# Feed-forward with blockwise rounding: weights rounded inside the expert loop, norm and input by quarters, pair loop written out

## The reference

```python
def fp4_quant_dequant(x):                 # blocks of 16 along the last axis
    scale = max(max(abs(xb)) / 6, 1e-12)
    idx = searchsorted(_MID, abs(xb / scale))
    return _GRID[idx] * sign(xb / scale) * scale
def fp4_linear(x, w): return einsum('bsk,nk->bsn', quant(x), quant(w))
x = x + ga * linear_attention(h)
h = layernorm(x) * (1 + cb) + sb
gate = fp4_linear(h, w_gate)              # w_gate, w_up: 352 x 128
y = fp4_linear(h, w_up)
x = x + gb * fp4_linear(silu(gate) * y, w_down)   # w_down: 128 x 352
```

## Time and profile before

| what | value |
|---|---|
| median of 3 runs | 1143.52 us (1142.25 to 1144.01) |
| the profiled execution | 1143.78 us |
| its span | 1142.0 us |
| PE busy | 884.3 us (77%) |
| DVE busy | 734.3 us (64%) |
| ACT busy | 453.7 us (40%) |
| POOL busy | 411.9 us (36%) |
| chain that ended last | PE 46%, DVE 23%, DMA 7%, POOL 7%, SP queue 6%, ACT 5%, issue 5% |

### The profile page before, as it was taken

One profiled execution on the slowest core, in us unless ns is written; L12 is line 12 of the kernel. 1 busy time (PEld: TensorE's weight loads), 2 busy tenths in 40 slices (PEclk: granted clock), 3 DMA queues, 4 the chain that ended last, 5 costly groups with the idle time before them and its releaser, 6 DMA issues.

```text
span 1142.0 us, 22164 instructions
## 1 busy us (share of the span) xinstructions
PE 884.3 (77%) x8587; PEld 671.1 (59%) x8587; DVE 734.3 (64%) x1571; ACT 453.7 (40%) x748; POOL 411.9 (36%) x447
## 2 busy tenths in 40 slices
PE   2484679999999999874689989999937850467774
PEld 1243668888888888653356656666615840254553
DVE  6683426555555655336687887888858768876664
ACT  4850123333333333245545565655633223222221
POOL 5552003333334333245223353334442056223232
PEclk8696889999999999896799999999978985578776
DMA  7075112233233323620000000000000000000000
GB/s 132 0 191 169 41 35 58 65 91 72 62 85 74 70 60 92 160 53 3 1 1 2 1 2 1 1 1 1 1 0 1 1 20 0 0 9 10 18 18 18
DMA packets 69608, 46.37 MB, mean 41 GB/s; under 512 B 35056, under 2 KB 60856, under 8 KB 68792
## 3 DMA queue, kind: packets, MB, share of 16 engines
q1 hardware_dynamic: 52776, 24.75, 9.7%
q0 software_dynamic: 8032, 19.11, 6.4%
q10 hardware_dynamic: 8704, 1.19, 0.6%
HBM read 30.05 MB, written 12.06 MB: 37 GB/s over the span
## 4 chain that ended last, share of the span: by engine, by line
PE 46%; DVE 23%; DMA 7%; POOL 7%; SPq 6%; ACT 5%; issue 5%; ACTq 0%; POOLq 0%; DVEq 0%
PE PS L1029 7%; PE PS L1125 5%; PE PS L1126 5%; PE PS L1127 5%; PE PS L1049 4%; PE PS L1009 3%; PE PS L1033 3%; PE PS L1010 3%; PE PS L1261 2%; SPq L336 2%; PE PS L1277 2%; DMA REG<-inverse_sums 2%; DVE HB L1682 2%; DVE REG L1479 2%; ACT REG L687 1%
## 5 line engine op out<-in xcount | busy, mean ns | idle before, releaser
L1460 DVE TENSOR_REDUCE MX<-PS 128x2 f32<-128x512 f32 x256 | 171.4, 686 | 172.2 <-PE PS L1010 170.6
L766 ACT ACTIVATE REG<-PS 128x1024 f32<-128x1024 f32 x128 | 131.5, 1027 | 242.2 <-PE PS L1033 239.4
L1029 PE MATMUL PS<-XX,TB 96*128 96x64 f16 x2048 | 160.0, 246 | 7.3 <-DMA XX<-NEG 4.5
L1009 PE MATMUL PS<-TM,YY 128*128 128x256 f16 x512 | 129.8, 285 | 32.8 <-DMA YY<-REG 15.2
L1029 PEld LDWEIGHTS PS<-XX,TB 96*128 96x128 f16 x2048 | 133.5, 120 | 22.8 <-issue 12.8
L608 POOL TENSOR_TENSOR HH<-HB,HH 128x512 f16<-128x512 f32 x64 | 75.6, 1181 | 171.2 <-ACT HH L813 171.2
L1010 PE MATMUL PS<-KM,YY 128*128 128x256 f16 x512 | 126.8, 279 | 0.0
L1682 DVE SCALAR_TENSOR_TENSOR HB<-PS,SG 128x512 f32<-128x512 f32 x128 | 87.5, 684 | 50.7 <-ACT SG L841 50.7
L841 ACT ACTIVATE SG<-PS 128x512 f32<-128x512 f32 x128 | 76.2, 595 | 110.3 <-PE PS L1127 110.0
L1033 PE MATMUL PS<-XX,KC 97*128 97x128 f16 x1024 | 107.8, 229 | 0.0
L1125 PE MATMUL PS<-XH,XX 128*128 128x512 f16 x256 | 98.8, 386 | 9.1 <-DVE HB L1682 8.9
(11 more groups left out here) (235 smaller groups left out, 1704.3 us busy)
## 6 DMA issues: line engine op xcount, KB each, us to landing
REG<-inverse_sums POOLq DMA_DIRECT2D x60, 128.0 KB, 2.9
YY<-queries_content ACTq DMA_DIRECT2D x224, 4.0 KB
KC<-keys_strips SPq DMA_DIRECT2D x16, 192.0 KB
keys_strips<-REG POOLq DMA_DIRECT2D x12, 224.0 KB, 8.0
R<-in_L_attn_x SPq DMA_DIRECT2D x32, 64.0 KB, 3.4
out<-R SPq DMA_DIRECT2D x64, 32.0 KB, 1.6
queries_position<-REG POOLq DMA_DIRECT2D x2, 960.0 KB, 12.9
queries_content<-REG POOLq DMA_DIRECT2D x2, 960.0 KB, 17.7
```

Of the source, the lines that this page charges most:

```text
L766: A(P[jt][:, 1024 * up:1024 * up + 1024].rearrange("p (k x) -> p k x", k=2), ST[u % 2], ACT.Exp).then_inc(exp_done, 1)
L1009: mm(o, yp[:, a], TM[p][:, 31 - a:31 - a + T], start=True, stop=False)
L1029: mm(o_pos[:, a], TB[p][0:96, y0:y0 + 128], xp[0:96, 8 * bank + a], start=(a == 0), stop=False, skip_group_check=True)
L1460: nc.vector.tensor_reduce(MX[h % 2][:, 2 * kk:2 * kk + 2], banks[4 + kk % 2].rearrange("p (a j) -> p a j", a=2), AX_X, ALU.max)\
```

## The change

- FN, WGU, WD1 and buffers for rounding the weights move into parts of YY that are free once layer 0's attention is done. GpSimd clears FN after the last normalise of attention, and SP loads the weights then instead of after layer 1's attention.
- VectorE rounds the weights in 16 pieces beside the expert loop (ten in block 1 from step 6, six in block 3 from step 10). TensorE transposes them in block 4 (steps 2 and 8) into banks 6 and 7, ScalarE copies them out (steps 6 and 10).
- Statistics, root, centring, scaling and shift go by quarters of eight tiles; VectorE now does the shift too. The input of quarters 0 and 1 is rounded ahead of the pairs, that of 2 and 3 in pieces between the steps of the first pairs.
- The input tiles are transposed two at a time within the pair loop, into bank 7, and go straight from there to XT; R1 isn't used.
- The pair loop is written out on all engines. TensorE's order is gate_and_up(m+1), hidden_transposes(m-1), down(m-2), input_transposes(m+3). HT has two buffers, both down products of a pair lie in bank 6, and GpSimd does output(m-3) behind scale_hidden(m).

The diff, cut (lines "# sync" and so on name the engine):

```diff
+        FN = YY[:, 3 * N + 1800:3 * N + 1800 + 2 * (768 + FF)].bitcast(F32)
+        YF = YY[:, 0:3 * N].bitcast(F32)
...
-        FN = sb("FN", [128, 6 * 128 + FF], F32, ff)
-        WGU = sb("WGU", [128, 2, FF], F32, ff)
-        WD1 = sb("WD1", [128, 3, 128], F32, ff)
-        HT = sb("HT", [128, 2, 3, 128], F32, ff)
+        HT = [sb(f"HT{j}", [128, 2, 3, 128], F32, ff) for j in range(2)]
 # sync
-            sp.wait_ge(l_od, 8)
             sp.wait_ge(zeroed, 15)
...
-            with sp.Fori(0, NT // 4) as c:
+            for c in range(NT // 4):
 # gpsimd
             for h in range(H - 1):
                 sums_to_dram(h)
                 normalise(h)
+            gp.wait_ge(max_mm, 16 * H)
+            gp.memset(FN, 0.0).then_inc(zeroed, 1)
...
-            residual(l_mul, R2, [CT[j][:, :] for j in range(2)], l_od)
-            gp.wait_ge(l_od, 8)
-            gp.memset(FN[:, :], 0.0).then_inc(zeroed, 1)
-            inverse_root(5)
-            shifted(3, HN3, MOD[1][:, 3, :], pre_ready)
...
-            scale_hidden(0, 0)
-            with gp.Fori(0, PAIRS // 2 - 1) as c:
-                for v in range(2):
-                    scale_hidden(2 * c + v + 1, 1 - v)
-                    output(2 * c + v, v)
-            scale_hidden(PAIRS - 1, 1)
-            output(PAIRS - 2, 0)
-            output(PAIRS - 1, 1)
+            for q in range(4):
+                linear_residual(2 * q)
+                linear_residual(2 * q + 1)
+                if q:
+                    quarter_root(5, q - 1)
+            quarter_root(5, 3)
+            scale_input(0)
+            scale_input(1)
+            for m in range(PAIRS):
+                scale_hidden(m)
+                if m in (2, 5):
+                    scale_input(2 + m // 5)
+                if m >= 3:
+                    output(m - 3)
+            for m in range(PAIRS - 3, PAIRS):
+                output(m)
 # scalar
+                elif tc == 4 and k in (6, 10):
+                    feed_weights(k // 4 - 1)
...
+            def stationary(m):
+                v = m % 2
+                act.wait_ge(f_xtr, m + 1)
+                if m >= 2:
+                    act.wait_ge(f_gu, m - 1)
+                A(XT[v][:, :, :], banks[7][:, 0:256].rearrange("p (u t) -> p u t", u=2), ACT.Copy).then_inc(f_xt, 1)
...
+            for q in range(3):
+                centre_tiles(5, HN3, range(8 * q, 8 * q + 8))
+            stationary(0)
+            stationary(1)
+            centre_tiles(5, HN3, range(24, 32))
             silu_gate(0)
+            stationary(2)
+            for m in range(PAIRS + 2):
                 if m + 1 < PAIRS:
                     silu_gate(m + 1)
+                if 1 <= m <= PAIRS:
+                    evacuate_hidden(m - 1)
+                if m >= 2:
+                    evacuate_output(m - 2)
                 if m + 3 < PAIRS:
+                    stationary(m + 3)
 # tensor
+                elif tc == 4 and k in (2, 8):
+                    feed_transposes(k // 8)
...
+            def input_transposes(m):
+                pe.wait_ge(h_ready, 24 + 2 * (m // 4) + 2)
+                if m:
+                    pe.wait_ge(f_xt, m)
+                for u in range(2):
+                    last = tr(banks[7][:, 128 * u:128 * u + 128], XQ[:, 2 * m + u, :], ident)
+                last.then_inc(f_xtr, 1)
...
-            with pe.Fori(0, PAIRS // 2 - 1) as c:
-                for v in range(2):
-                    gate_and_up(2 * c + v + 1, 1 - v)
-                    hidden_and_down(2 * c + v, v)
+            pe.wait_ge(l_mul, 8)
+            input_transposes(0)
+            input_transposes(1)
+            gate_and_up(0)
+            input_transposes(2)
+            for m in range(PAIRS + 2):
+                if m + 1 < PAIRS:
+                    gate_and_up(m + 1)
+                if 1 <= m <= PAIRS:
+                    hidden_transposes(m - 1)
+                if m >= 2:
+                    down(m - 2)
+                if m + 3 < PAIRS:
+                    input_transposes(m + 3)
 # vector
+            def feed_weights():
+                ve.wait_ge(ld_ff, 80)
+                for part, (lo, nb) in enumerate(((0, 48), (768, FF // 16))):
+                    w = FN[:, lo:lo + 16 * nb].rearrange("p (k s) -> p k s", s=16)
+                    t = [b[:, 0:16 * nb].rearrange("p (k s) -> p k s", s=16) for b in (WS0, WS1)]
+                    if part:
+                        ve.wait_ge(f_w, part)
+                    yield from quantised(w, t[0], t[1], [v[:, 0:nb] for v in WAM], norm, f_wround)
+                    ve.wait_ge(f_wround, part + 1)
+                    TT(w, t[0], WAM[2][:, 0:nb].unsqueeze(2).to_broadcast([128, nb, 16]), ALU.mult).then_inc(f_w, 1)
+                    yield
...
+                elif tc == 1 and k >= 6 or tc == 3 and k >= 10:
+                    next(weights)
...
-            scaled(3, HN3, MOD[1][:, 4, :])
...
+            def hidden(m):
+                v = m % 2
+                ve.wait_ge(f_sg, m + 1)
+                if m >= 2:
+                    ve.wait_ge(f_ht, m - 1)
+                elif m == 1:
+                    ve.wait_ge(h_ready, 24 + 4)
+                TT(HQ[v][:, :, :], SGP[:, :, :], gate_up[:, :, 1], ALU.mult).then_inc(f_h, 1)
+                yield
+                ve.wait_ge(f_h, m + 1)
+                yield from quantised(HQ[v][:, :, :].rearrange("p u (k s) -> p (u k) s", s=16), *pair_buffers[v][0:2],
+                                     pair_buffers[v][2:], hidden_step, f_round)
...
             for c in range(4):
+                linear_gate(c)
+            for _ in feed_statistics(0):
+                pass
+            for c in range(4, 6):
+                linear_gate(c)
+            for _ in feed_statistics(1):
+                pass
+            for c in range(6, 8):
+                linear_gate(c)
+            for piece in (feed_norm(0), feed_statistics(2), feed_input(0), feed_norm(1), feed_statistics(3), feed_input(1)):
+                for _ in piece:
+                    pass
+            behind = itertools.chain(feed_norm(2), feed_input(2), feed_norm(3), feed_input(3))
+            for m in range(PAIRS):
+                for _ in hidden(m):
+                    next(behind, None)
```

More of the change, by code:

```diff
@@ L7 @@
+import itertools
 from contextlib import ExitStack
@@ L705, in projected @@
                 A(*natural(c, 0), ACT.Identity, bias=VEC3[:, kind:kind + 1]).then_inc(high_done, 1)
-            def centre(k, src, dst, done, before=0):
-                for n in range(NT):
-                    if n % (NT // 2) == 0:
-                        act.wait_ge(rstd_ready, 17 + n // (NT // 2))
-                    last = A(dst[:, n, :], src[:, n, :], ACT.Identity, bias=LN[:, 3, n:n + 1], scale=LN[:, 2, n:n + 1])
-                    if n % 4 == 3:
-                        last.then_inc(done, 1)
             for q in range(3):
@@ L950, in _, with transposes @@
             tr(banks[7][:, 0:128], WN[:, 4, :], ident).then_inc(pe_prep, 1)
[L952 to L960 removed]
+            def transposes(c):
+                pe.wait_ge(h_ready, c + 1)
+                if c >= 2:
+                    pe.wait_ge(t_evac, c - 1)
+                for j in range(4):
+                    last = tr(banks[4 + c % 2][:, 128 * j:128 * j + 128], HN[:, 4 * c + j, :], ident)
+                last.then_inc(t_done, 1)
             def project(c):
@@ L1111, in linear_transposes, with feed_transposes @@
                 last.then_inc(t_done, 1)
+            def feed_transposes(part):
+                pe.wait_ge(f_w, part + 1)
+                if part == 0:
+                    pe.wait_ge(t_evac, 16 + 2)
+                    for w in range(2):
+                        for c in range(3):
+                            m = (128, 128, 96)[c]
+                            last = tr(banks[6 + w][:, 128 * c:128 * c + m], FN[0:m, 384 * w + 128 * c:384 * w + 128 * c + 128],
+                                      ident[0:m, 0:m])
+                else:
+                    pe.wait_ge(f_ev, 1)
+                    for c in range(3):
+                        m = (128, 128, 96)[c]
+                        last = tr(banks[6][0:m, 128 * c:128 * c + 128], FN[:, 768 + 128 * c:768 + 128 * c + m], ident)
+                last.then_inc(f_tr, 1)
             def logits(half):
@@ L1316, in statistics @@
                 STT(var, var, 1.0 / D, t, ALU.mult, ALU.add).then_inc(var_ready, 1)
-            def scaled(order, dst, scale):
-                for c in range(8):
-                    ve.wait_ge(centred, 8 * order + c + 1)
-                    t = dst[:, 4 * c:4 * c + 4, :]
-                    TT(t, t, scale.unsqueeze(1).to_broadcast([128, 4, D]), ALU.mult).then_inc(scale_done, 1)
             norm = Later(ve, norm_dve)
@@ L1787, in _ @@
-            for half in range(2):
-                ve.wait_ge(l_od, 4 * half + 4)
-                statistics(R2, half_tiles(half))
-            ve.wait_ge(ld_ff, 80)
-            for lo, nb in ((0, 48), (768, FF // 16)):
```

(5 more changed lines are left out.)

253 lines of the change are left out of this document (96 added, 157 removed).

## The result

| kernel | median, us | its runs | ratio to before |
|---|---|---|---|
| before, beside it | 1143.22 | 1142.25 to 1144.01 | |
| after | 1100.86 | 1099.39 to 1102.54 | 0.963 [0.9612, 0.9649] |
| after, once more (a1_changed_again) | 1100.18 | 1099.49 to 1100.66 | 0.9625 [0.9611, 0.9639] |

The change makes the kernel 3.7% faster; forecast were 1103.5 us and a range of 1095 to 1120. The profiled execution took 1102.54 us, its span is 1100.7, 41.3 less than the 1142.0 of before. To see where they come from, both traces are cut at the same five events on VectorE: first and last hidden product of the expert loop, first gate product of linear attention, first product of pair 0, and end of the last rounding step.

The account below looks back on a forecast made before the run. Hand-overs, not an engine, were taken to bound the feed-forward. Pair 0 at 965.4, loop 119.2 + 1.5 and tail 13.6 end at 1099.7; expert loop +2.3 gives span 1102.0, plus 1.8 less 0.3: 1103.5 us, range 1095 to 1120.

Parts of the forecast that it names:

- What bounds it: Feed-forward: bound by hand-overs, not by an engine; VectorE waits about 4.6 us in every second pair.
- Start of the feed-forward: First gate product to pair 0 on VectorE: pair 0 starts at 965.4 instead of 997.97, 32.6 us earlier.
- contention term of 1.5: Ahead of pair 0: 1.5 us added to VectorE's work for GpSimd's residual adds and roots beside it.
- ScalarE's last centring and its table load (till 964.3) hide below that product: Before pair 0: ScalarE's work ends under the first gate and up product, so it adds nothing.
- Loop: Pair 0 to last rounding: pairs 99 us, late pieces 17.8, late scalings 2.4, low clock 1.5.
- The late scalings: Pair loop: GpSimd's two late quarter scalings hit one pair each, 1.2 us apiece, 2.4 together.
- Tail: Last rounding to end: 13.6 us with TensorE at full clock instead of 14.8; 16.5 at the low clock.
- Expert loop: Weight rounding and transposes put into the expert loop lengthen it by 2.3 us: 1.1 from pieces, 1.2 from transposes.
- The nine weight transposes are pure addition on the bound engine: Expert loop: weight transposes on TensorE add their full time, 1.2 us.
- (a): Rival, pair loop: GpSimd and VectorE block each other fully, pairs 8.6 us, 1134; half a step's drift 1113; chance 0.12.
- (b): Rival, pair loop: TensorE stays at 1.2 GHz and becomes the bound, 10.0 us per pair, 1135 in all; chance 0.10.
- (c): Rival, expert loop: added pieces open TensorE waits that lower its clock, making the kernel slower, 1150 or more; chance 0.03.
- (d): Rival, pair loop: order fails, VectorE still waits in each second pair, half the loop's gain lost, 1125; chance 0.05.

Follow-up runs that it names:

- a1_changed_again: The changed kernel once more, unedited, beside a version with three further edits on the same chip: 1100.18 us, ratio 0.9625.
- e1: Changed kernel with TensorE's transposes and down product of a pair back in the earlier two-deep order, ScalarE and GpSimd following: 1130.96 us in one run.
- e2: Changed kernel with all 16 weight-rounding pieces, transposes and copies behind the last gate product instead of beside the expert loop: 1108.31 us, ratio 0.9702.
- e4: Changed kernel with input quarters 2 and 3 scaled, shifted and rounded ahead of pair 0 too: 1103.85 us, ratio 0.9648.
- e6: Changed kernel with GpSimd scaling input quarter 0 before the root of quarter 3 instead of behind it: 1097.57 us in one run.
- e3: Changed kernel with the late quarters' 22 pieces in groups of eight behind whole pairs instead of one after each step: 1108.95 us, ratio 0.9707.
- e8: Changed kernel with weight pieces only behind even expert-loop steps over blocks 1 to 5, transposes in block 5: 1095.02 us in one run.
- e5: Changed kernel without GpSimd's multiplication of the outputs by the gate: 1099.46 us in one run.
- e9: Changed kernel with quarter 0 scaled before the last root, last two outputs by VectorE from PSUM, and weight pieces behind even steps only: 1092.64 us, ratio 0.9559.

## Why the prediction was right, and where it was off

- **What bounds it.** Hand-overs and no engine: right. VectorE's busy time is nearly equal in both traces, and e1 brings its waits back with nothing but the order. Of the 31.1 us won ahead of pair 0, e2 shows 8.7 (the weights) and e4 18.0 (quarters 2 and 3, of which 13.6 come back in the pairs); the other 4.3 (norm by quarters, the shift on VectorE, input straight to XT) no run takes apart.
- **Start of the feed-forward, 42.8 forecast, 44.3 measured.** The chain was the forecast one (last root, quarter scaling, transposes, gate product, SiLU; e6 shortens it at the root). The last root starts 32.9 us after the first gate product, 1.8 later than the forecast's 31.1. The contention term of 1.5 was too small: the two shifts at 942.60, beside GpSimd's residual adds, take 3.47, where the next two take 1.29, so they alone cost 2.2, and two of the 128x8 steps of the statistics, at 937.76 and 938.24, take 0.48 and 1.24 instead of 0.17. From the root to pair 0 it is 11.4 us, forecast 11.7, and there two errors cancel: the first gate and up product takes 3.57 instead of 5.06, but "ScalarE's last centring and its table load (till 964.3) hide below that product" failed: because of them SiLU starts 1.43 us after the product's end. The step at 962.25 (2.98, under the quarter scaling) is off the path: VectorE waits 3.29 us behind it.
- **Loop, 120.7 forecast, 113.3 measured: the term that was off most.** Steady pairs were right: 6.11 against 6.24, the rest being a rounding step that takes 1.01 under the residual add, not 1.13. The late scalings, forecast 1.2 each, cost 1.1 and 1.5 (pairs of 7.20 and 7.61 us). The first three pairs with their 22 pieces, forecast 37.2 (17.9 of pairs, 17.8 of pieces, 1.5 of low clock), took 31.2. I had added durations of steps that each wait for the one before. Alternating, pairs and pieces take 4.5 us less than their sum of 35.7, and the 1.5 for the low clock wasn't needed (from 980 to 1000 the clock is 0.62, and VectorE is busy 20.00 of 20 us). Without alternating, in e3, it takes 39.65. What the forecast had at nothing is the contribution of steps of two chains.
- **Tail, 13.6 forecast, 15.6 measured.** The forecast took TensorE at full clock, with 16.5 for the low one. The clock was 0.52 there; the low-clock end was the nearer one. What I had missed is that TensorE, once the gate and up products are through, waits over 2 us for each scaling of the last two pairs, and that the last down product waits 0.56 for the evacuation of pair 14's from the same bank.
- **Expert loop, +2.3 forecast, +3.1 measured.** Right in size, wrong in one part. "The nine weight transposes are pure addition on the bound engine" holds only for block 4 (1.28 us, forecast 1.2); e8 shows them at 0.09 in block 5. And of the 2.2 us that VectorE was reckoned to get over its slack, 1.65 reached TensorE instead of 1.1, while the same pieces behind even steps, in e8, cost 0.16.
- **Before the expert loop, 0 forecast, +1.8 measured.** This stretch varied by 6 us over executions whose kernels are the same there, so no cause is given.
- **The sum.** 1102.0 forecast for the span plus 1.8 + 0.8 + 1.5 - 7.4 + 2.0 gives 1100.7. The forecast's nearness owes something to terms that cancel: the loop's surplus pays for four smaller shortfalls.
- **Rivals.** (a) Full mutual blocking: the mechanism is real (e5, e3), its place in the steady pair harmless, 0.25 + 0.12 us; the phases are kept since VectorE sets them. (b) The low clock: 1.00 from 1040 to 1060 in spite of a wait of 1.3 us in each pair; from 1020 to 1080 it came nowhere, only in the tail. (c) The expert loop lost 3 us, not 40. (d) The order does what it says. Without it (e1) the loop is 26.0 us longer. The span is 28.4 longer: 4.1 more lie ahead of the first gate product, where no edit is, and 1.7 less at pair 0 and in the tail.

Not settled: e2 and the changed kernel differ by 7.4 us in the medians and by 5.8 in the two stretches that the edit touches. Another 0.8 lies between the expert loop and the gate product, a stretch that varies by 3 us over the runs; the rest is open. And e1 and e5 to e8 were timed once each: their verdicts rest on stretches, and those of e6 to e8 on e9's five runs too.

## What to carry to other kernels

When one engine's steps depend on each other, lay the steps of a second, independent chain between them: here the hand-overs got 3.5 us cheaper over 46 steps, and contention 5.0, and adding durations up overestimated the result. On an in-order engine put the consumer of a far hand-over one or two items later than the producer's turn: without that order the buffers and the unrolling brought nothing to the loop, with it 25.9 us. Whether the order would work without the second buffer wasn't tried. Read the slack of each step before laying work beside a loop: the same pieces and transposes cost 3.1 us where there was none and 0.25 a few steps further on.

## What the runs showed of the hardware that I had not expected

- **A waiting step starts later than one whose input is old.** In the changed kernel, the scaling at 972.58 starts 0.08 us before the product's end (971.77 + 0.89 = 972.66), and the reduction at 973.18 again 0.08 before the scaling's; the reciprocal at 1012.49, which needs the scaling before it, starts 0.03 after. This 0.11, met behind 34 of the 46 instructions in e3 and behind hardly any in the changed kernel, makes most of the 3.5 us of hand-overs. The Trainium skill, VectorE: DVE Perf Modes, section "The DRAIN you can't avoid", says that the next operation doesn't start until the pipe is empty, that one which isn't held starts earlier, and that a semaphore after each operation added nothing in its measurement. The starts 0.08 us early agree with the second; against the third, an instruction that waits on the one just before it starts 0.11 us later here.
- **A blocked instruction has part of its start behind it.** The step at 1012.95, held until the add ended at 1013.21, ended 0.75 later, where it takes 0.89 unhindered.
- **TensorE's clock against waits.** With waits of 1.29 us in each pair of 6.1 us it stayed at full speed, 1.00, that is 2.4 GHz (window 1040 to 1060). Behind the waits of 2.09 and 2.26 us it fell, and the last window, at 0.52, is nearly all at 1.2 GHz. In e1, with 0.95 in each pair and 2.38 in every second one besides, the mean is 0.80.
- **The smallest operation can be hit hardest.** 128x44 elements took 1.65 us instead of 0.19, under a quarter scaling of 1.94.
